# A fused attention and MLP block: the next chunk's normed rows are turned by VectorE's 32 by 32 blocks and DRAM transfers instead of TensorE transposes

## The chip, the cores and the metric

The kernel runs on one core of a Trainium2 chip. The metric is the device time of one execution in microseconds, lower is better, as the median of several runs. The profile and trace are of one further execution. Engines: TensorE (PE; its weight loads are PEld), VectorE (DVE), ScalarE (ACT), GpSimd (POOL), SyncE (SP), which here only issues DMA transfers.

## The reference

A sandwich-normed transformer block in float32: 16 sequences of 256 tokens, model width 256, 16 heads of 128, MLP width 2048. The MLP's weights come as four-bit codes with scales. Cut to what matters:

```python
def _layernorm(x, axis=-1, eps=1e-05):
    m = jnp.mean(x, axis=axis, keepdims=True)
    v = jnp.var(x, axis=axis, keepdims=True)
    return (x - m) / jnp.sqrt(v + eps)

# attention
q = jnp.einsum('bpd,hde->bphe', x, W_Q) + b_Q          # k, v alike
scores = jnp.einsum('bqhe,bkhe->bhqk', q, k) / ATTN_SCALE
attn = jax.nn.softmax(jnp.where(causal, scores, IGNORE), axis=-1)
out = jnp.einsum('bqhe,hed->bqd', jnp.einsum('bkhe,bhqk->bqhe', v, attn), W_O) + b_O
# MLP
Wg, Wu, Wd = (dequant_nvfp4(packed, scales) for each of gate, up, down)
gate, up = xt @ Wg.T, xt @ Wu.T
out = (gelu_tanh(gate) * up) @ Wd.T
# block
x = x + _layernorm(_L0_attn_ref(_layernorm(x, axis=-1), ...), axis=-1)
x = x + _layernorm(_L0_ffn_ref(_layernorm(x, axis=-1), ...), axis=-1)
```

## The kernel before

**Tiling.** The 4096 tokens are 8 chunks of 512 (two sequences each). All chunks pass through attention first, then all through the MLP; between them each chunk's result x1 lies in DRAM (`x1_scratch`, written from the tile `stream`). Every float32 product is three float32r products, hi x hi, hi x lo and lo x hi, so each operand is split: ACT writes the hi part (a rounded copy), DVE or POOL the lo part (value minus hi). Each projection of one head on one chunk is 6 matmuls of 512 columns (L752 to L754, helper `three`).

**Steps.** Attention is 128 steps, n = 16 c + j: chunk c, head j. `step_plan(n)` is the order in which TensorE works in a step: q and k of head n+1, the output projection of head n-3 ("out"), the weighted values of head n-2 ("z"), the scores of head n+1; and in steps with j % 4 = 1 the four banks of V (v0 to v3) for the next four heads. Such a step is called a V step here, the others short. ACT, DVE and POOL follow the same list with their own halves, each engine strictly in its order. The PSUM banks of q, k, z and v are three in a ring (`fbank`): a product can only start when the one three places before it has been split.

**The way of the probabilities.** After softmax (masks by DVE, exponentials by ACT, reciprocals by DVE, scaling by POOL), DVE turns head n's probabilities in 32 by 32 blocks ("T", line 1134, tile `turned`). SP sends `turned` to DRAM (`send`, L514), waits until it has landed, and loads it back as four DMAs in a turned layout (`fetch`, L524, tile `back`). In step n+1 ACT makes the hi part of it ("pT", L708, tile `pT_hi`) and only then the exponentials of head n+2, since its list says so; the lo part is POOL's, and TensorE uses both in step n+2. SP has one list for all transfers and stands still at each wait.

**Work hung between.** Around the steps DVE does other things in the gaps, set by tables: `X1_AT` for the norm and residual of the chunk before (its result `given` is turned by DVE blocks and by a DRAM round trip too, SP's `turn_given` at j = 5), `NEXT_AT` for the norm of the next chunk's rows (`norm_next_x`), and `spread` for the decoding of one piece of MLP weights in the steps named in `W4_SLOTS` (48 pieces in all; ACT, POOL and SP take part, with four DMAs in the step after). A place (j, "sum") is after step j's scores have been masked and z split and the sums inverted; (j, "end") is after the last V bank.

**The next rows before.** The rows of chunk c+1 are loaded to `x_in` (SP, j = 3 and 5), get their statistics at j = 10 and 12 and are normed into `stream` at (13, "end"), which has to wait until SP's stores of x1 out of `stream` (j = 11 and 13) have landed. In step 14 TensorE transposes them ("xT", L771: two groups of four transposes of 128x128 into PSUM, one before and one after "out"), ACT writes `xnT_hi` (L620) and DVE `xnT_lo` (L932). The q projection in step 15 reads them.

## Time and profile before

| | |
|---|---|
| median of 3 runs | 1577.87 us (1573.5 to 1579.29) |
| the profiled execution, whole time | 1580.88 us |
| its span in the trace | 1579.1 us |
| PE busy | 1549.9 us, 98% |
| DVE, ACT, POOL busy | 1071.8, 981.7, 711.2 us |
| DMA | 183.13 MB, mean 116 GB/s |

The attention steps take up the first 1040 us or so of the span, the MLP the rest. The profiled execution took 1580.88 us, 3.0 us above the median of the timed runs; 1.8 us of it lie outside the span. Matmuls overlap: one of 512 columns is shown with 0.39 us, but the next one starts 0.23 us after it, so lengths of PE work are read here from starts.

### The profile page before, as it was taken

The page shows a single profiled execution, that of the slowest core. Times are in us where ns is not written, and L with a number is a line of the kernel's source. Part 1 is how long each engine was busy: PE and PEld are TensorE (multiplying, and loading weights), DVE is VectorE, ACT ScalarE, POOL GpSimd, SP SyncE. Part 2 cuts the span into 40 slices and gives each one's busy share as a digit, 9 for nine tenths or more (in the row PEclk, how much of TensorE's full clock was granted, in tenths as well). Part 3 has the DMA queues.
Part 4 walks back from the last instruction along what each step waited for, and adds up shares of the span by engine and source line. Part 5 has one row for each costly group of instructions (what it writes and reads, how often), then busy time and mean ns, then how long its engine had stood idle before and what let it go on. Part 6 is the DMA issues. An engine that isn't in the chain of part 4 may idle for free.

```text
span 1579.1 us, 25677 instructions
## 1 busy us (share of the span) xinstructions
PE 1549.9 (98%) x8160; PEld 1332.4 (84%) x8160; DVE 1071.8 (68%) x3088; ACT 981.7 (62%) x2449; POOL 711.2 (45%) x1069
## 2 busy tenths in 40 slices
PE   6999999999999999999999999999999999999998
PEld 5888888888888888888888888887888888888887
DVE  5666677677777778667767766756666566565665
ACT  6887667767776776777776776653444444444443
POOL 5774445445554545445544543333333333333333
PEclk9999999999999999999999999999999999999999
DMA  4653444444454354444444455481101101111001
GB/s 135 188 169 114 142 137 145 146 155 137 139 173 134 124 172 135 145 156 131 141 152 144 146 162 159 155 289 52 43 26 54 41 28 42 38 54 41 27 28 40
DMA packets 168375, 183.13 MB, mean 116 GB/s; under 512 B 17328, under 2 KB 139696, under 8 KB 168240
## 3 DMA queue, kind: packets, MB, share of 16 engines
q1 hardware_dynamic: 168240, 181.50, 36.0%
q8 instruction: 65, 1.06, 0.3%
q14 instruction: 70, 0.57, 0.1%
HBM read 102.26 MB, written 79.17 MB: 115 GB/s over the span
## 4 chain that ended last, share of the span: by engine, by line
PE 79%; DMA 7%; SPq 4%; DVE 4%; ACT 4%; issue 2%; POOL 1%; DVEq 0%
PE fbank L752 13%; PE fbank L754 13%; PE fbank L753 13%; PE obank L752 6%; PE obank L754 6%; PE obank L753 6%; PE ubank L752 5%; PE ubank L754 5%; PE ubank L753 5%; DMA turned_scratch<-turned 3%; PE ubank L776 3%; PE fbank L854 2%; SPq L524 2%; DMA back<-turned_scratch 2%; ACT probs L640 1%
## 5 line engine op out<-in xcount | busy, mean ns | idle before, releaser
L752 PE MATMUL fbank<-xnT_hi,wqk_hi 128*128 128x512 f32 x768 | 301.2, 392 | 1.1 <-DVE xnT_lo L932 1.1
L753 PE MATMUL fbank<-xnT_lo,wqk_hi 128*128 128x512 f32 x768 | 300.2, 391 | 0.0
L754 PE MATMUL fbank<-xnT_hi,wqk_lo 128*128 128x512 f32 x768 | 299.8, 390 | 0.0
L1327 POOL TENSOR_TENSOR pT_lo<-back,pT_hi 128x512 fp32r<-128x512 f32 x128 | 165.8, 1295 | 290.6 <-ACT pT_hi L708 290.6
L651 ACT ACTIVATE w_raw<-fbank 128x512 f32<-128x512 f32 x128 | 76.5, 598 | 230.6 <-PE fbank L754 230.5
L1289 POOL TENSOR_SCALAR probs<-probs,rsum 128x128 f32<-128x128 f32 (+1 forms) x512 | 208.8, 427 | 14.5 <-DVE rsum L955 10.5
L947 DVE CUSTOM_DVE_ANT_0 probs<-ubank,mask 128x128 f32<-128x128 f32 (+1 forms) x512 | 155.9, 355 | 25.3 <-PE ubank L754 24.1
L754 PEld LDWEIGHTS fbank<-xnT_hi,wqk_lo 128*128 128x128 f32 x768 | 144.7, 188 | 30.8
L752 PEld LDWEIGHTS fbank<-xnT_hi,wqk_hi 128*128 128x128 f32 x768 | 145.4, 189 | 28.7 <-DVE xnT_lo L932 1.5
L753 PEld LDWEIGHTS fbank<-xnT_lo,wqk_hi 128*128 128x128 f32 x768 | 145.0, 189 | 25.7
L1307 POOL TENSOR_TENSOR v_lo<-probs,v_hi 128x512 fp32r<-128x512 f32 x64 | 82.4, 1288 | 166.0 <-ACT v_hi L660 166.0
L1071 DVE SCALAR_TENSOR_TENSOR probs<-w_raw,fbank 128x512 f32<-128x512 f32 x128 | 88.1, 688 | 98.3 <-ACT w_raw L655 95.9
L621 ACT ACTIVATE zT_hi<-fbank,bias_v 128x512 fp32r<-128x512 f32 x128 | 87.4, 683 | 101.8 <-PE fbank L854 101.8
L1065 DVE SCALAR_TENSOR_TENSOR w_raw<-w_raw,fbank 128x512 f32<-128x512 f32 x128 | 87.7, 685 | 86.9 <-ACT w_raw L651 85.8
L1307 POOL TENSOR_TENSOR kT_lo<-probs,kT_hi 128x512 fp32r<-128x512 f32 x64 | 82.9, 1296 | 134.1 <-ACT kT_hi L660 134.1
L934 DVE SCALAR_TENSOR_TENSOR kT_lo<-fbank,bias_k,kT_hi 128x512 fp32r<-128x512 f32 x128 | 95.9, 749 | 54.3 <-ACT k_early L632 53.6
L1134 DVE STREAM_TRANSPOSE turned<-probs 128x384 f32<-128x384 f32 x256 | 131.6, 552 | 0.6 <-DMA turned_scratch<-turned 0.6
L640 ACT ACTIVATE probs<-probs,nmax 128x256 f32<-128x256 f32 x256 | 126.7, 495 | 0.0
L655 ACT ACTIVATE w_raw<-w_raw 128x512 f32<-128x512 f32 x128 | 80.9, 632 | 47.6 <-DVE w_raw L1065 47.6
L955 DVE RECIPROCAL rsum<-sums 128x2 f32<-128x2 f32 x256 | 41.7, 163 | 100.2 <-ACT probs L640 99.7
L776 PE MATMUL ubank<-k_early,q_early 128*128 128x128 f32 x512 | 102.2, 281 | 7.2 <-DVE kT_lo L934 6.5
L638 ACT ACTIVATE probs<-probs,nmax 128x128 f32<-128x128 f32 x256 | 100.3, 392 | 9.8 <-DVE nmax L947 6.7
(144 smaller groups left out, 4288.4 us busy)
## 6 DMA issues: line engine op xcount, KB each, us to landing
turned_scratch<-turned SPq DMA_DIRECT2D x128, 384.0 KB, 2.6
back<-turned_scratch SPq DMA_DIRECT2D x512, 96.0 KB, 2.2
w_raw<-in_w_pairs SPq DMA_DIRECT2D x28, 256.0 KB, 3.0
w_hi_scratch<-w_hi SPq DMA_DIRECT2D x48, 128.0 KB, 2.0
w_lo_scratch<-w SPq DMA_DIRECT2D x48, 128.0 KB, 2.0
x_res<-in_x SPq DMA_DIRECT2D x16, 256.0 KB, 2.9
wqk_hi<-w_hi_scratch SPq DMA_DIRECT2D x16, 256.0 KB, 5.5
wqk_lo<-w_lo_scratch SPq DMA_DIRECT2D x16, 256.0 KB, 5.9
```

The lines of the kernel that those rows point to most:

```text
L638: act.activation(pr[:, 0:P], pr[:, 0:P], ACT.Exp, bias=nmax[:, 0:1], scale=-1.0, accum_out=sums[:, 0:1])
L640: act.activation(pr[:, P:384], pr[:, P:384], ACT.Exp, bias=nmax[:, 1:2], scale=-1.0, accum_out=sums[:, 1:2]).then_inc(s.exp, 1)
L752: nc.tensor.matmul(out, a[0], b[0], start=start, stop=False, skip_group_check=skip)
L753: nc.tensor.matmul(out, a[0], b[1], start=False, stop=False, skip_group_check=skip)
L754: return nc.tensor.matmul(out, a[1], b[0], start=False, stop=stop, skip_group_check=skip)
L776: nc.tensor.matmul(bank[:, 0:P], mem.q_early[i][:, b, :], mem.k_early[i][:, b, :], start=True, stop=True)
L934: ins = dve.scalar_tensor_tensor(dst, bank, bias, hi.bitcast(F32), ALU.add, ALU.subtract)
L947: last = dve.tensor_tensor_reduce(out=pr[:, lo:hi], in0=bank[:, lo:hi], in1=mask, scale=-SCALE, scalar=3.0e38, op0=ALU.add, op1=ALU.min, a ...
L1134: dve.transpose(mem.turned[:, :, :, b, :].rearrange("p k u j -> p u k j"), mem.probs[b].rearrange("p (u k j) -> p u k j", u=3, k=4)).then_ ...
L1289: last = pool.tensor_scalar(pr[:, lo:hi], pr[:, lo:hi], mem.rsum[i][:, at:at + 1], 1.0, ALU.mult, ALU.mult)
L1307: pool.tensor_tensor(lo, mem.act_v[j % 2], hi.bitcast(F32), ALU.subtract).then_inc(s.iT_lo, 1)
L1327: pool.tensor_tensor(lo[:].rearrange("p u b (a j) -> p (u b) a j", j=32), mem.back[m % 2][:, :, 0:2].rearrange("p a u b j -> p (u b) a j") ...
```

## The change

- The next chunk's rows are loaded earlier (both halves at j = 0), get their statistics at (1, "mid") and (2, "sum") and are normed in place in `x_in` at (4, "sum") and (5, "mid"), where "mid" is a new place between two V banks. In chunk 0 the first statistics are at (1, "end").
- At (6, "sum") DVE turns the normed rows in 32 by 32 blocks (`turn_rows`, four transposes of 128x256, whose source is read at a stride of two elements) into `w_raw` (chunk 0: `stream`). At j = 7 SP stores them to DRAM (512 KB), waits for the landing and loads them back to `x_in` as four DMAs of 128 KB. In step 14, after k, ACT writes `xnT_hi` and DVE `xnT_lo` from there; on DVE these two stand before T. TensorE's "xT" groups and their places in the ring of banks are gone from the attention steps. (The MLP's own transposes stay, and so do the eight of the kernel's start.)
- `turn_given` moves from j = 5 to j = 9 on SP, and `X1_AT` from places 3 to 9 to places 8 to 14; the x1 stores move from j = 11 and 13 to j = 15, both residual loads to j = 1 of the next chunk (the last chunk: j = 15).
- `W4_SLOTS` loses slot 15: seven pieces of MLP weights a chunk, so that the 48 reach into the last chunk; the loads of finished pieces wait for their own piece only.
- In the MLP's first chunk the parts of the attention's last norm and the roots that go with it stand one step later; the next rows' norm takes two steps instead of four.

The diff, cut to its core:

```diff
-W4_SLOTS = [1, 3, 5, 7, 9, 11, 13, 15]
-X1_ROOTS, NEXT_ROOTS = 9, 13
+W4_SLOTS = [1, 3, 5, 7, 9, 11, 13]
+X1_ROOTS, NEXT_ROOTS = 13, 3
...
     if n % HEADS == HEADS - 2:
-        plan += [("xT", 0)]
+        plan.insert(2, ("rows", n // HEADS + 1))
     if n > 2:
         plan += [("out", n - 3)]
-    if n % HEADS == HEADS - 2:
-        plan += [("xT", 1)]
     if n > 1:
...
+        self.first_stored = sem("first_x1_stored")
+        self.rows_turned = sem("rows_turned")
+        self.rows_sent = sem("turned_rows_stored")
+        self.rows_back = sem("turned_rows_back")
+        self.rows_hi = sem("rows_hi")
+        self.rows_lo = sem("rows_lo")
...
 def x1_norm(c):
-    return 2 * c + 2
+    return 2 * c + 3
 def next_norm(c):
-    return 2 * c + 3
+    return 2 * c + 2 if c else 3
...
-def load_program(sp, mem, s, x_v, w_pairs, biases, words_v, scales_v, w4_v, x1_v, turned_v, given_v, out_v):
+def stored_chunks(engine, s, chunks):
+    if chunks:
+        engine.wait_ge(s.first_stored, 32)
+    if chunks > 1:
+        engine.wait_ge(s.stored, 32 * (chunks - 1))
+def load_program(sp, mem, s, x_v, w_pairs, biases, words_v, scales_v, w4_v, x1_v, turned_v, given_v, rows_v,
+                 out_v):
...
-        sp.wait_ge(s.w4_stored, 32 * PIECES)
+        sp.wait_ge(s.w4_stored, 32 * (2 * unit + 2))
...
         if c:
-            sp.wait_ge(s.xn, c)
+            sp.wait_ge(s.rows_lo, KT * c)
         else:
         if c == NCH - 1:
-            sp.wait_ge(s.stored, 32 * (NCH - 2))
+            sp.wait_ge(s.first_stored, 32)
         src = part_of(x_v, c + 1, i) if c < NCH - 1 else part_of(x1_v, 0, i)
...
-                     mem.stream[:, i * half:(i + 1) * half]).then_inc(s.stored, 16)
+                     mem.stream[:, i * half:(i + 1) * half]
+                     ).then_inc(s.stored if c > 1 else s.first_stored, 16)
...
+    def turn_rows(n):
+        sp.wait_ge(s.rows_turned, 2 * n + 2)
+        if n:
+            sp.wait_ge(s.rows_back, 64 * n)
+        sp.dma_start(rows_v.rearrange("a i k c -> (a i) k c"),
+                     mem.rows_turned[min(n, 1)].rearrange("p k t r i -> p k (t r i)")
+                     ).then_inc(s.rows_sent, 16)
+        sp.wait_ge(s.rows_sent, 16 * (n + 1))
+        for k in range(4):
+            sp.dma_start(mem.rows_back[32 * k:32 * k + 32].rearrange("p a t r i -> p a (t r i)"),
+                         rows_v[:, :, k].rearrange("a i c -> i a c")).then_inc(s.rows_back, 16)
...
-        if c and j == 5:
+        if j == 7:
+            turn_rows(c)
+        elif c and j == 9:
...
                 w4_load(done + 1)
-        if j in (3, 5):
-            next_x(c, (j - 3) // 2)
-        elif c and j in (11, 13):
-            store_x1(c, (j - 11) // 2)
+        if j == 0:
+            for i in range(2):
+                next_x(c, i)
+        elif c and j == 1:
+            for i in range(2):
+                load_res(c - 1, i)
         elif j == 15:
-            load_res(c, 0)
-            if c == NCH - 1:
-                load_res(c, 1)
-        elif c and j == 1:
-            load_res(c - 1, 1)
+            for i in range(2):
+                if c:
+                    store_x1(c, i)
+                if c == NCH - 1:
+                    load_res(c, i)
         if c == NCH - 1 and j % HG == 1:
...
                 full(count, mem.zT[0][:], bank, mem.bias_v[:, h:h + 1]).then_inc(s.hi, 1)
-            else:
-                full(count, mem.xnT[0][:, m, :], bank).then_inc(s.hi, 1)
+        elif kind == "rows":
+            act.wait_ge(s.rows_back, 64 * m)
+            act.wait_ge(s.full, nth(("k", n + 1)))
+            for kt in range(KT):
+                act.activation(mem.xnT[0][:, kt, :].rearrange("p (t a i) -> p t a i", a=4, i=BLK),
+                               mem.rows_back[:, :, :, kt, :].rearrange("p a t i -> p t a i"),
+                               ACT.Copy).then_inc(s.rows_hi, 1)
         elif kind == "pT":
...
             act.wait_ge(s.out, m // HEADS + 1)
+            stored_chunks(act, s, m // HEADS)
             for i in range(2):
...
             if kind == "q" and h == 0:
-                pe.wait_ge(s.lo, split(("xT", m // HEADS, KT - 1)))
+                pe.wait_ge(s.rows_lo, KT * (m // HEADS))
             project(bank, h, 0 if kind == "q" else 1)
-        elif kind == "xT":
-            if m == 0:
-                pe.wait_ge(s.xn, c + 1)
-            transpose_x(mem.stream, m, bank).then_inc(s.full, 1)
         elif kind == "v":
...
         view = mem.given_turned[0 if n < NCH - 1 else 1]
-        if i == 0 and n == 0:
-            dve.wait_ge(s.w_split, len(PAIRS))
+        if i == 0 and n < NCH - 1:
+            dve.wait_ge(s.rows_sent, 16 * (n + 2))
         dve.transpose(view[:, :, :, i, :].rearrange("p a t j -> p t a j"),
...
             moments()
+        elif part == 5:
+            turn_rows(c)
         else:
             dve.wait_ge(s.rstd, next_norm(c))
-            if c:
-                dve.wait_ge(s.stored, c * 32)
-            last = standardise(xn, x_in, 2 * (part - 3))
-            if part == 4:
-                last.then_inc(s.xn, 1)
+            after(standardise(x_in, x_in, 2 * (part - 3)))
+    def turn_rows(n):
+        if n == 1:
+            dve.wait_ge(s.w_split, len(PAIRS))
+        for t in range(TT):
+            last = dve.transpose(mem.rows_turned[min(n, 1)][:, :, t].rearrange("p k r i -> p r k i"),
+                                 x_in[:, t, :].rearrange("p (k j r) -> p r k j", r=KT, j=BLK))
+            if t % 2:
+                last.then_inc(s.rows_turned, 1)
...
-    X1_AT = {(3, "sum"): (-2,), (4, "sum"): (-1,), (6, "sum"): (0,), (8, "sum"): (1, 2),
-             (9, "end"): (3, 4, 5, 6)}
-    NEXT_AT = {(10, "sum"): (0,), (12, "sum"): (1, 2), (13, "end"): (3, 4)}
+    X1_AT = {(8, "sum"): (-2, -1), (10, "sum"): (0,), (12, "sum"): (1, 2), (13, "mid"): (3, 4),
+             (14, "sum"): (5, 6)}
+    NEXT_AT = {(1, "mid"): (0,), (2, "sum"): (1, 2), (4, "sum"): (3,), (5, "mid"): (4,),
+               (6, "sum"): (5,)}
+    FIRST_NEXT_AT = {**NEXT_AT, (1, "end"): (0,)}
+        for part in (NEXT_AT if c else FIRST_NEXT_AT).get((j, place), ()):
+            norm_next_x(part, c)
-        for part in NEXT_AT.get((j, place), ()):
-            norm_next_x(part, c)
...
                     extra(c, j, "sum")
-            else:
-                full(count, mem.xnT[1][:, m, :], mem.xnT[0][:, m, :], bank)
+        elif kind == "rows":
+            for kt in range(KT):
+                dve.wait_ge(s.rows_hi, KT * (m - 1) + kt + 1)
+                dve.tensor_tensor(mem.xnT[1][:, kt, :].rearrange("p (t a i) -> p t a i", a=4, i=BLK),
+                                  mem.rows_back[:, :, :, kt, :].rearrange("p a t i -> p t a i"),
+                                  mem.xnT[0][:, kt, :].bitcast(F32).rearrange(
+                                      "p (t a i) -> p t a i", a=4, i=BLK),
+                                  ALU.subtract).then_inc(s.rows_lo, 1)
         elif kind == "T":
...
-            for part in {4: (-1,), 7: (0, 1), 8: (2, 3), 9: (4, 5)}.get(m, ()):
+            for part in {4: (-1,), 8: (0, 1), 9: (2, 3), 10: (4, 5)}.get(m, ()):
-        if 7 <= j < 11 and c < NCH - 1:
-            norm_next_y(j - 7, c)
+        first = 7 if c else 9
+        if j in (first, first + 1) and c < NCH - 1:
+            for part in (0, 1):
+                norm_next_y(2 * (j - first) + part, c)
...
                 w4_lo(piece)
+            if j == NEXT_ROOTS:
+                roots(next_norm(c))
             if c and j == X1_ROOTS:
                 roots(x1_norm(c))
-            if j == NEXT_ROOTS:
-                roots(next_norm(c))
         elif kind == "pT":
```

SP's list around the turned rows, chunk 1, from the last DMA of step 6 to the first of step 8's weight piece (`turned_scratch<-turned` is a send, `back<-turned_scratch` a fetch). Before:

```order
L500 DMA scale<-in_scales 128x1x128
L514 DMA turned_scratch<-turned 128x768
L524 DMA back<-turned_scratch 32x4x192 x4
L514 DMA turned_scratch<-turned 128x768
L524 DMA back<-turned_scratch 32x4x192 x4
L506 DMA w_hi_scratch<-w_hi 128x256
```

And in the changed kernel:

```order
L521 DMA scale<-in_scales 128x1x128
L535 DMA turned_scratch<-turned 128x768
L545 DMA back<-turned_scratch 32x4x192 x4
L566 DMA rows_scratch<-w_raw 128x1024
L571 DMA x_in<-rows_scratch 32x4x256 x4
L535 DMA turned_scratch<-turned 128x768
L545 DMA back<-turned_scratch 32x4x192 x4
L527 DMA w_hi_scratch<-w_hi 128x256
```

The store and the four loads of the rows now stand between the fetch of head 7 and the send of head 8.

DVE's list in step 14 of chunk 1, from q's lo part to the first mask of the scores. Before:

```order
L934 SCALAR_TENSOR_TENSOR qT_lo<-fbank,bias_q,qT_hi 128x256
L934 SCALAR_TENSOR_TENSOR kT_lo<-fbank,bias_k,kT_hi 128x512
L1134 STREAM_TRANSPOSE turned<-probs 128x3x4x32 x2
L932 TENSOR_TENSOR xnT_lo<-fbank,xnT_hi 128x512 x2
L947 ISA probs,nmax<-ubank,mask 128x128
```

And in the changed kernel:

```order
L975 SCALAR_TENSOR_TENSOR qT_lo<-fbank,bias_q,qT_hi 128x256
L975 SCALAR_TENSOR_TENSOR kT_lo<-fbank,bias_k,kT_hi 128x512
L1180 TENSOR_TENSOR xnT_lo<-x_in,xnT_hi 128x512 x2
L1190 STREAM_TRANSPOSE turned<-probs 128x3x4x32 x2
L988 ISA probs,nmax<-ubank,mask 128x128
```

The two lo parts of the next rows moved ahead of the turning of head 14's probabilities.

## Rows read from the trace of the kernel before

**Rows 1.** The page's first part: busy time, share, instructions by engine.
```profile
PE 1549.9 (98%) x8160; PEld 1332.4 (84%) x8160; DVE 1071.8 (68%) x3088; ACT 981.7 (62%) x2449; POOL 711.2 (45%) x1069
```

**Rows 2.** Timeline, PE: start us, length, engine, line, op, tiles, shape, count.
```profile
128.02 0.39 PE L752 MATMUL fbank<-xnT_hi,wqk_hi 128*128 128x512 f32 x1
...
130.75 0.63 PE L771 MATMUL fbank<-ident,stream 128*128 128x128 f32 x4
...
135.39 0.40 PE L752 MATMUL fbank<-xnT_hi,wqk_hi 128*128 128x512 f32 x1
...
1019.41 0.39 PE L752 MATMUL fbank<-xnT_hi,wqk_hi 128*128 128x512 f32 x1
```

**Rows 3.** Timelines of PE, DVE, SP's queue and ACT, chunk 7 steps 9 to 11.
```profile
976.49 0.40 PE L752 MATMUL fbank<-xnT_hi,wqk_hi 128*128 128x512 f32 x1
...
988.35 0.39 PE L752 MATMUL fbank<-xnT_hi,wqk_hi 128*128 128x512 f32 x1
...
993.02 1.03 DVE L1134 STREAM_TRANSPOSE turned<-probs 128x384 f32<-128x384 f32 x2
...
994.08 0.32 SPq L514 DMA_DIRECT2D turned_scratch<-turned  x1
...
994.75 0.39 PE L752 MATMUL fbank<-xnT_hi,wqk_hi 128*128 128x512 f32 x1
...
996.47 1.75 SPq L524 DMA_DIRECT2D back<-turned_scratch  x4
...
1000.78 0.62 ACT L708 ACTIVATE pT_hi<-back 128x512 fp32r<-128x512 f32 x1
```

**Rows 4.** The page's DMA issues: count, KB each, median us from issue to landing.
```profile
back<-turned_scratch SPq DMA_DIRECT2D x512, 96.0 KB, 2.2
```

**Rows 5.** Waits: engine, tile, line, releaser: total us, times, longest.
```profile
DVE stream L970 <- DMA x_scratch<-stream: 8.0, 7, 2.0
```

**Rows 6.** A group of DVE by form: count | busy us, mean ns | idle before.
```profile
L1134 DVE STREAM_TRANSPOSE turned<-probs 128x384 f32<-128x384 f32 x256 | 131.6, 552 | 0.6 <-DMA turned_scratch<-turned 0.6
```

**Rows 7.** Timeline of SP's queue, chunk 1: `turn_given` at step 5, then head 6.
```profile
192.12 0.42 SPq L533 DMA_DIRECT2D given_scratch<-w_raw  x1
195.16 1.73 SPq L537 DMA_DIRECT2D w_raw<-given_scratch  x4
...
197.59 0.34 SPq L514 DMA_DIRECT2D turned_scratch<-turned  x1
201.34 1.74 SPq L524 DMA_DIRECT2D back<-turned_scratch  x4
```

**Rows 8.** Timelines of ACT and PE, chunk 1, V step 5 with a late `back`.
```profile
186.71 0.63 ACT L708 ACTIVATE pT_hi<-back 128x512 fp32r<-128x512 f32 x1 [0.90 <-DMA back<-turned_scratch]
...
190.36 0.50 PE L752 MATMUL fbank<-wv_hi,xnT_hi 128*128 128x512 f32 x1
```

**Rows 9.** PE after three idle times; three windows: us, PE busy, PEclk, DMA share, GB/s.
```profile
37.62 0.80 PE L776 MATMUL ubank<-k_early,q_early 128*128 128x128 f32 x2 [2.01 <-DVE kT_lo L934]
...
975.23 0.49 PE L776 MATMUL ubank<-k_early,q_early 128*128 128x128 f32 x2 [1.34 <-DVE kT_lo L934]
...
1075.04 0.61 PE L752 MATMUL obank<-v_hi,wv_hi 128*128 128x512 f32 x1 [2.28 <-POOL v_lo L1307]
...
38.00:40.00 2.00, 2.00 (x11) 0.50 0.65 210
40.00:42.00 2.00, 2.00 (x8) 0.76 0.82 222
...
976.00:978.00 2.00, 2.00 (x13) 1.00 0.49 197
```

**Rows 10.** Timeline of DVE, first MLP chunk: the attention's last norm.
```profile
1070.32 1.54 DVE L987 BATCH_NORM_STATS2 stats<-back 128x6 f32<-128x256 f32 x4 [3.54 <-DMA back<-given_scratch]
```

**Rows 11.** Timelines of SP's queue and DVE, chunk 0, steps 0 and 1.
```profile
26.78 1.75 SPq L524 DMA_DIRECT2D back<-turned_scratch  x4
...
31.66 1.03 DVE L1134 STREAM_TRANSPOSE turned<-probs 128x384 f32<-128x384 f32 x2
```

More of the change, by code:

```diff
@@ L149, in full_key @@
 def full_key(n, kind, m):
-    if kind == "xT":
-        return (kind, n // HEADS + 1, m)
     if kind == "v":
@@ L281, in __init__, with blocks @@
                              for v in places]
+        def blocks(view):
+            return view.rearrange("p (k t r i) -> p k t r i", t=TT, r=KT, i=BLK)
+        self.rows_turned = [blocks(self.stream[:].rearrange("p t d -> p (t d)")), blocks(raw)]
+        self.rows_back = blocks(self.x_in[:].rearrange("p t d -> p (t d)"))
         def bank(name, shape):
@@ L767, in project, with transpose_x @@
         last.then_inc(s.full, 1)
-    def transpose_x(src, kt, bank):
+    def transpose_x(kt, bank):
         for t in range(TT):
-            last = nc.tensor.transpose(bank[:, t * P:(t + 1) * P], src[:, t, kt:D:KT], mem.ident[:])
+            last = nc.tensor.transpose(bank[:, t * P:(t + 1) * P], mem.x_in[:, t, kt:D:KT],
+                                       mem.ident[:])
         return last
@@ L871, in tensor_program @@
             if m == 0:
-                pe.wait_ge(s.lo, split(("xT", NCH, KT - 1)))
+                pe.wait_ge(s.rows_lo, KT * NCH)
             if m < 2:
@@ L1111, in vector_program @@
             if whole(kind, m):
-                if m == TT - 1:
-                    extra(c, j, "end")
+                extra(c, j, "end" if m == TT - 1 else "mid")
                 continue
@@ L1336, in pool_program @@
             inter_lo(c * NT + m - 1, m - 1)
-            if m == (7 if c == 0 else 4):
+            if m == (8 if c == 0 else 4):
                 roots(y_norm(c))
-            elif j == 8 and c < NCH - 1:
+            elif j == (7 if c else 9) and c < NCH - 1:
                 roots(y_next_norm(c))
```

13 lines of the change are left out of this document (7 added, 6 removed).

## The prediction

> **What bounds the kernel now.** The busy shares come first: TensorE is busy 98% of the span [rows 1], so time can only be won by giving it less to do or by closing what is left of its gaps. Next come the starts of its steps in PE's timeline. A short step takes 994.75 - 988.35 = 6.40 us, a V step 988.35 - 976.49 = 11.86 [rows 3]. Step 14, with the transposes, takes 135.39 - 128.02 = 7.37 [rows 2]. A chunk without any waiting would be 12 x 6.40 + 4 x 11.86 + 0.97 = 125.2 us; it is (1019.41 - 128.02) / 7 = 127.3 [rows 2]. So each chunk loses 2.1 us to stalls, 15 us in seven chunks. The third thing to read is how close the other queues run behind TensorE. In step 10 of chunk 7 DVE ends T 5.70 us after the step's start, SP sends at 5.73, fetches from 8.12 to 9.87, and ACT begins pT_hi in the next step at 1000.78 - 994.75 = 6.03 [rows 3]. A fetch lands 2.2 us after its issue [rows 4]; the last of the four is issued at about 9.4, so `back` is there at 11.6, that is 5.2 in the next step: **0.8 us of slack** for the whole way through DRAM. In a short step ACT has nothing to spare behind pT_hi, so more delay than that reaches TensorE one step later, less the time by which k's lo part is early, which I estimate at 0.4 us from the starts of the scores.
>
> In a V step there is more room, since the V banks follow. In chunk 1 step 5 pT_hi came at 186.71, late by a landing, and the fourth V bank, which waits for the first to be split, at 190.36, 3.65 later [rows 8]. Undisturbed it begins six matmuls before the step's end. Twelve take 130.75 - 128.02 = 2.73 [rows 2], six 1.36, so it begins at 11.86 - 1.36 = 10.50. Hence pT_hi may be as late as **6.85** in a V step; beyond that TensorE stalls one for one.
>
> **The change, part by part** (against the profiled execution, 1580.9 us).
>
> *Transposes gone.* 7.37 - 6.40 = 0.97 us for the eight of a chunk [rows 2, 3], eight chunks: **-7.8**. The rows show about 0.12 us for each transpose. The Trainium skill (TensorE: Matmul & The Clock Gate, part 4 on PE-mode transpose) gives about 275 ns for one in a kernel's context; by that the 64 would be worth 17.6 us and the sum 9.8 us lower. The measurement decides, so 0.12 stands.
>
> *Norms spread evenly.* The wait of the norm for the landing of x1's stores (8.0 us of DVE in seven chunks [rows 5]) has no cause left, since the rows are normed in place; it stood just ahead of step 14. The double loads on DVE (a turn of `given` beside a spread) are parted. What stays are the pieces of weights, seven a chunk, with four DMAs each in SP's list. I take it that of 15 us some 5 stay: **-10**, bounds -4 and -13.
>
> *Step 14.* On DVE the two lo parts (128x512; in proportion to the 0.552 us of 384 columns [rows 6] some 0.7 us each) now precede T, so T and the masks are 1.3 us late, and with them the exponentials. Behind the masks follow two residual adds of the same size, 1.4 us. DVE idles 32% of the time [rows 1], 2.0 us of a short step, and I count half of it ahead of k's lo part: 1.3 + 1.4 less 1.0 leaves this late by some 1.2 to 1.7, less 0.4. I take **+0.8** a chunk, eight chunks **+6.4**, bounds +2 and +11.
>
> *Step 6.* Four block transposes of 256 columns. One of 384 takes 0.552 [rows 6]; in proportion 0.37, at most the same 0.55: 1.5 to 2.2 us. The same 1.0 of idle time takes most of it, and k has 0.4: nothing on TensorE, but T of step 7 ends up to 0.3 late.
>
> *Steps 7 to 9: SP's list.* This is the term that decides. `turn_rows` stands behind fetch 7 and ahead of send 8, and a short step has no time for it. Its price is that of `turn_given`, same bytes, same form: 195.16 - 192.12 = 3.04 us from the store's issue past its landing, 1.73 for four loads, and the send that follows closely behind such loads takes 201.34 - 197.59 = 3.75 until its fetch can start, where a quiet one takes 2.39 [rows 7, 3]. Before, this stood in V step 5, whose extra 5.45 us hid it. Now, from step 7's start: T 6.0, send, landed after 2.4 to 2.9 (step 6's weight piece is on the queue), fetch issued until 10.6, store, loads from 13.65 to 15.4. That is 9.0 in step 8, where the send was due at 5.73. Landed at 12.75, `back` there 3.5 later (1.75 of issues, 2.2 of landing, less one issue) at 16.2: 9.8 in step 9. All quiet it would be 8.6. Step 9 is a V step, so TensorE stalls at its fourth bank by 9.8 - 6.85 = 2.95, quiet by 1.75. I take 2.8, in eight chunks **+22.4**, bounds +14 and +27.
>
> *The clock behind that stall.* After idle times of 2.01 and 2.28 us TensorE worked at half its clock (0.50, which is 1.2 GHz; window 38 to 40), after 1.34 us it stayed at full (1.00, 2.4 GHz; window 976 to 978) [rows 9]. A gap of 2.7 us is on the falling side. The window 40 to 42 has a mean of 0.76, so the half clock ended at 41.0; 41.0 - 37.6 = 3.4 us at half cost 1.7 us. In seven of eight chunks: **+11.9**, bounds 0 and +13.6.
>
> *Last chunk.* At j = 9 `turn_given` meets four loads of finished weights, as at j = 5 before, where the send of head 6 was held up and the stall at 975.23 followed [rows 9]. It moves rather than goes; as I counted it among the 15, it comes back: **+2**.
>
> *MLP start.* DVE waited 3.54 us for `given` [rows 10]; POOL's roots waited for DVE and TensorE 2.28 us for POOL, then ran at half clock [rows 9]. One MLP step is 18 matmuls, 4.1 us, more than the wait. One step later it is gone: 2.4 + 1.7 = **-4.1**, bounds 0 and -4.1.
>
> *Kernel start.* In chunk 0 the first statistics stand at (1, "end"), ahead of T. Their rows are issued only after the fetch that ends at 28.5, two issues of 0.45, and a landing of some 3 us; T began at 31.66 [rows 11]. With 0.8 of statistics T comes 1.4 later, on a way that already stalls TensorE at 37.62: **+1.4**, bounds 0 and +2.
>
> **Sum.** -7.8 - 10 + 6.4 + 22.4 + 11.9 + 2 - 4.1 + 1.4 = +22.2: the profiled execution would be 1603.1. It lay 3.0 above the median of the runs, so the median goes to **1600 us**, 1.4% slower.
>
> **The rivals.**
>
> *The clock stays up.* For it: a third idle time, of 1.34 us, left it at full, and only two cases speak for the fall, both at other places. Against it: both were shorter than the gap here. Without the 11.9 the median is **1588**; with the quiet stall of 1.75 instead, 1580.
>
> *SP's list is no bound.* If the rows' round trip were hidden, say because `back` of head 8 has more slack than I read, the stall, the clock and the last chunk's collision fall out: 1600 - 22.4 - 11.9 - 2 = **1564**, and the change does what its name says. For it: the DMA engines are far from full (0.49 of their time in a window of the attention steps [rows 9]), and the same round trip cost nothing at step 5. Against it: SP waits for a landing, which more bandwidth doesn't shorten, and at step 5 the V banks hid it. The stall begins where `back` of head 8 is more than 6.85 - 5.2 = 1.65 us late; I count 9.8 - 5.2 = 4.6.
>
> *The turns are dear.* If the strided source doubles the four block transposes to 3 us, k's lo part is late by 1.9, TensorE stalls 1.4 us more in step 7 and the way to send 8 grows: +11 us, **1611**. No row shows a strided turn. The Trainium skill (SBUF - State Buffer, door 1 on the DMA port swizzle) says that float32 reads within a 16-byte line keep full bandwidth, and a stride of two elements stays within; by it the price is the lower one, which is the one I took.
>
> **How the numbers follow.** Forecast (stall and half clock) 0.50; clock stays up 0.25; SP no bound 0.13; turns dear 0.12. The forecast with its own bounds reaches from about 1590 to 1609. The range takes in the clock rival and half of the dear turns: 1581 to 1611; what is left out is mostly the fast case. Within 0.5% of before (about what a measurement of this kernel can tell from no change) is 1570 to 1586: a part of the clock rival with quiet landings, 0.08. Faster 0.13, slower 0.79.
>
> **What would show it.** In the changed trace: SP's queue sends head 8 about 3 us later than 5.73 after step 8's start, in every chunk; ACT's pT_hi in step 9 waits for `back` near 9.8; the fourth V bank of step 9 has 2.5 to 3 us of idle time before it, released by DVE's v_lo, with PEclk at 0.50 behind it, eight times; step 14 is 6.4 long and step 15 about 7.2; the wait on x1's stores is gone and the idle time near 1075 too. I am wrong if pT_hi of step 9 starts before 6.9, or if the clock stays at 1.00 behind the stalls, or if new waits stand elsewhere, such as in step 7 by the turns.

## The result, and the profile after

| | before | after |
|---|---|---|
| median of four runs, us | 1578.58 (1573.50 to 1580.58) | 1608.49 (1603.62 to 1609.48) |
| profiled execution, whole / span, us | 1580.88 / 1579.1 | 1603.62 / 1601.8 |
| mean granted clock of TensorE | 0.996 | 0.992 |

The ratio is 1.0188, with a 95% interval of 1.0156 to 1.0220: the change costs 25 to 35 us. Its profiled execution was the fastest of its four; the spans of the two traces differ by 22.7 us.

The page of the changed kernel, first and fourth part (busy times, and the chain that ended last):

```profile
PE 1550.4 (97%) x8096; PEld 1327.8 (83%) x8096; DVE 1082.2 (68%) x3120; ACT 981.6 (61%) x2449; POOL 718.9 (45%) x1069
...
PE 67%; DMA 12%; SPq 6%; ACT 6%; DVE 5%; issue 2%; POOL 0%; DVEq 0%; ACTq 0%
```

TensorE has 64 matmuls fewer than in [rows 1] and as much busy time, because some of its matmuls ran at half clock. Transfers (DMA) and SP's queue (SPq) now hold 18% of the chain, which was 11% before. PE's waits (engine, tile, line, releaser: total us, times, longest) say where:

```profile
PE fbank L796 <- DVE v_lo L973: 21.5, 10, 3.3
PE ubank L821 <- DVE kT_lo L975: 9.8, 15, 4.3
```

A V bank waited for `v_lo` ten times, 21.5 us in all; before, no row of this view had that wait. One of the ten, from step 7 to step 9 of chunk 1 (steps begin at 205.09, 211.50 and 217.91), in the timelines of PE, SP's queue and ACT:

```profile
205.09 0.39 PE L796 MATMUL fbank<-xnT_hi,wqk_hi 128*128 128x512 f32 x1
...
211.50 0.39 PE L796 MATMUL fbank<-xnT_hi,wqk_hi 128*128 128x512 f32 x1
...
217.91 0.39 PE L796 MATMUL fbank<-xnT_hi,wqk_hi 128*128 128x512 f32 x1
...
231.75 0.50 PE L796 MATMUL fbank<-wv_hi,xnT_hi 128*128 128x512 f32 x1 [2.73 <-DVE v_lo L973]
```

```profile
210.82 0.32 SPq L535 DMA_DIRECT2D turned_scratch<-turned  x1
213.33 3.30 SPq L545 DMA_DIRECT2D back<-turned_scratch  x4
216.72 0.38 SPq L566 DMA_DIRECT2D rows_scratch<-w_raw  x1
219.48 1.73 SPq L571 DMA_DIRECT2D x_in<-rows_scratch  x4
221.31 0.38 SPq L535 DMA_DIRECT2D turned_scratch<-turned  x1
224.48 1.73 SPq L545 DMA_DIRECT2D back<-turned_scratch  x4
```

```profile
228.10 0.63 ACT L751 ACTIVATE pT_hi<-back 128x512 fp32r<-128x512 f32 x1 [4.07 <-DMA back<-turned_scratch]
```

Step 7 takes 211.50 - 205.09 = 6.41 us and head 7 is sent 5.73 into it: the turns on VectorE delay nothing. In step 8 SyncE fetches head 7, stores the rows, stands for their landing until 219.48, issues four loads, and sends head 8 at 221.31, which is 9.81 after the start of step 8. `back` releases pT_hi at 228.10, 10.19 into step 9, and the fourth V bank starts 3.65 later, as in [rows 8]: 3.34 us late.

The differences between the two traces' starts of TensorE's steps, summed over the chunks, against the terms of the prediction ("late T" is its term for step 14):

| steps | the prediction's terms, us | measured, us |
|---|---|---|
| 14 to 1 of the next chunk | -7.8 transposes, +6.4 late T: -1.4 | -1.4 (14 and 15: -6.5; 0 and 1: +5.1) |
| 4 to 13 | -10 spread, +22.4 stall, +11.9 clock, +2 last chunk: +26.3 | +22.7 (4 to 8: -6.4; 9 and 10: +29.0) |
| kernel start | +1.4 | +3.0 |
| MLP | -4.1 | -1.6 |
| sum | +22.2 | +22.7 |

The clock. PE in chunks 2 and 5, and windows (us, PE busy, PEclk, DMA share, GB/s) behind the stalls of chunks 1, 2 and 5:

```profile
363.03 0.50 PE L796 MATMUL fbank<-wv_hi,xnT_hi 128*128 128x512 f32 x1 [2.58 <-DVE v_lo L973]
...
752.57 0.50 PE L796 MATMUL fbank<-wv_hi,xnT_hi 128*128 128x512 f32 x1 [3.29 <-DVE v_lo L973]
```

```profile
232.00:234.00 2.00, 2.00 (x7) 0.58 0.52 150
...
363.00:365.00 2.00, 1.97 (x9) 1.00 0.52 149
365.00:367.00 2.00, 2.00 (x10) 1.00 0.71 263
...
754.00:756.00 2.00, 2.00 (x10) 1.00 0.93 338
```

TensorE fell to 1.2 GHz behind the idle time of 2.73 us and stayed at 2.4 GHz behind one of 2.58, and in chunk 5 behind one of 3.29. In this execution it fell in four of eight chunks, for 3.4 us each time, which costs 1.7.

The kernel start (DVE, then PE), step 14 of chunk 1 (PE, then DVE), and the MLP (DVE, PE, POOL):

```profile
33.37 0.75 DVE L1001 BATCH_NORM_STATS2 stats<-x_in 128x6 f32<-128x256 f32 x2 [3.01 <-DMA x_in<-in_x]
...
40.12 0.80 PE L821 MATMUL ubank<-k_early,q_early 128*128 128x128 f32 x2 [4.35 <-DVE kT_lo L975]
```

```profile
265.93 0.39 PE L796 MATMUL fbank<-xnT_hi,wqk_hi 128*128 128x512 f32 x1
...
272.34 0.46 PE L796 MATMUL fbank<-xnT_hi,wqk_hi 128*128 128x512 f32 x1
...
270.76 1.42 DVE L1180 TENSOR_TENSOR xnT_lo<-x_in,xnT_hi 128x512 fp32r<-128x512 f32 x2
272.10 1.02 DVE L1190 STREAM_TRANSPOSE turned<-probs 128x384 f32<-128x384 f32 x2
```

```profile
1097.19 1.54 DVE L1028 BATCH_NORM_STATS2 stats<-back 128x6 f32<-128x256 f32 x4 [1.76 <-DMA back<-given_scratch]
...
1115.91 0.47 PE L796 MATMUL obank<-v_hi,wv_hi 128*128 128x512 f32 x1 [1.45 <-POOL v_lo L1365]
...
1113.24 0.19 POOL L1312 TENSOR_SCALAR var_eps<-mv 128x4 f32<-128x4 f32 x1 [3.58 <-DVE mv L1006]
```

VectorE stood 3.01 us for the first rows, with head 1's T queued behind, and TensorE idled 4.35 us at 40.12 where it idled 2.01 before [rows 9]. Step 14 is 6.41 long instead of 7.37, but T ends at 273.12, 7.19 after its start. In the MLP the wait for `given` went from 3.54 [rows 10] to 1.76, and TensorE's stall at 1075 went with the half clock behind it; 0.53 us is left, at 1101.94. A new stall stands at 1115.91, where GpSimd stood for the moments of the next rows with TensorE's `v_lo` queued behind.

### The profile page after: what moved, and what is told of

Its sections match the earlier page's. It is cut to its first block, busy times and chain, and to the rows that moved or that the text cites. A ratio compares the mean times of both kernels' runs of the same rounds, so it can differ in the third digit from the quotient of the medians.

```text
span 1601.8 us, 25642 instructions
## 1 busy us (share of the span) xinstructions
PE 1550.4 (97%) x8096; PEld 1327.8 (83%) x8096; DVE 1082.2 (68%) x3120; ACT 981.6 (61%) x2449; POOL 718.9 (45%) x1069
## 4 chain that ended last, share of the span: by engine, by line
PE 67%; DMA 12%; SPq 6%; ACT 6%; DVE 5%; issue 2%; POOL 0%; DVEq 0%; ACTq 0%
PE fbank L796 12%; PE fbank L798 12%; PE fbank L797 12%; DMA turned_scratch<-turned 6%; PE obank L796 5%; PE obank L798 5%; PE obank L797 5%; PE ubank L798 4%; PE ubank L796 4%; PE ubank L797 4%; SPq L545 3%; DMA back<-turned_scratch 3%; PE ubank L821 2%; PE fbank L895 2%; ACT probs L678 2%
## 5 line engine op out<-in xcount | busy, mean ns | idle before, releaser
L1347 POOL TENSOR_SCALAR probs<-probs,rsum 128x128 f32<-128x128 f32 (+1 forms) x512 | 216.6, 444 | 21.8 <-DVE rsum L996 18.0
L988 DVE CUSTOM_DVE_ANT_0 probs<-ubank,mask 128x128 f32<-128x128 f32 (+1 forms) x512 | 155.3, 354 | 24.7 <-PE ubank L798 22.7
L797 PEld LDWEIGHTS fbank<-xnT_lo,wqk_hi 128*128 128x128 f32 x768 | 146.1, 190 | 26.3
L796 PE MATMUL fbank<-wv_hi,xnT_hi 128*128 128x512 f32 x256 | 102.2, 399 | 23.4 <-DVE v_lo L973 21.5
L751 ACT ACTIVATE pT_hi<-back 128x512 fp32r<-128x512 f32 x128 | 80.2, 626 | 58.3 <-DMA back<-turned_scratch 57.6
```

The lines of the kernel that those rows point to most:

```text
L796: nc.tensor.matmul(out, a[0], b[0], start=start, stop=False, skip_group_check=skip)
L797: nc.tensor.matmul(out, a[0], b[1], start=False, stop=False, skip_group_check=skip)
L988: last = dve.tensor_tensor_reduce(out=pr[:, lo:hi], in0=bank[:, lo:hi], in1=mask, scale=-SCALE, scalar=3.0e38, op0=ALU.add, op1=ALU.min, a ...
L1347: last = pool.tensor_scalar(pr[:, lo:hi], pr[:, lo:hi], mem.rsum[i][:, at:at + 1], 1.0, ALU.mult, ALU.mult)
```

## The experiments

Each time is a median with the ratio to the kernel before, run beside it.

**The loads one step later.** The changed kernel, with this edit. SyncE's wait for the landing moves too, as it stands just ahead of the loads.

```diff
                     ).then_inc(s.rows_sent, 16)
+
+    def rows_home(n):
         sp.wait_ge(s.rows_sent, 16 * (n + 1))
         for k in range(4):
...
             turn_rows(c)
+        elif j == 8:
+            rows_home(c)
         elif c and j == 9:
```

> The changed kernel, but SyncE stores the turned rows in step 7 as before and issues their four loads one step later, behind fetch 8, by when the store has long landed: nothing is left that SyncE waits for between fetch 7 and send 8. The same bytes move. If the landing that SyncE stands for (and the loads behind it) makes send 8 late, send 8 goes from 9.8 us after its step's start to about 5.8, step 9 of every chunk falls from some 15.3 us to 11.9, and 27.9 us of stall with the half clock behind it go, less what the loads in step 8 add to head 8's fetch (they stand behind it; up to 0.3 us a chunk for send 9): 1605 - 26 = about 1579 to 1582. The rival, that it is the added bytes or VectorE's added turns that make head 8 late, expects step 9 to stay above 14 us and the time above 1600.

1587.4 us, ratio 1.0043 (1.0029 to 1.0058). SP's queue, ACT and PE of chunk 1:

```profile
214.03 0.34 SPq L535 DMA_DIRECT2D turned_scratch<-turned  x1
...
222.39 0.63 SPq L535 DMA_DIRECT2D turned_scratch<-turned  x1
...
230.22 1.73 SPq L558 DMA_DIRECT2D w_raw<-given_scratch  x4
232.12 0.34 SPq L535 DMA_DIRECT2D turned_scratch<-turned  x1
236.50 1.73 SPq L545 DMA_DIRECT2D back<-turned_scratch  x4
```

```profile
239.97 0.63 ACT L755 ACTIVATE pT_hi<-back 128x512 fp32r<-128x512 f32 x1 [1.05 <-DMA back<-turned_scratch]
```

```profile
226.38 0.39 PE L800 MATMUL fbank<-xnT_hi,wqk_hi 128*128 128x512 f32 x1
...
245.26 0.49 PE L825 MATMUL ubank<-k_early,q_early 128*128 128x128 f32 x2 [0.66 <-DVE kT_lo L979]
```

Step 9 is 11.9 us in all chunks: the whole stall of step 9 went, with the bytes unchanged. So what SyncE does between fetch 7 and send 8, the wait and the four loads together, made it, and the rival (bytes, or the turns) is out. The time was forecast at 1579 to 1582 and is some 6 us longer, because the next wait came forward: steps 11 to 13 of chunks 1 to 7 are 12.5 us longer than before. The send of head 10 (232.12, 5.74 into step 10) goes right behind the loads of `given` and its fetch starts only 4.38 us later; that makes pT_hi late in step 11 and TensorE idle in step 12. In the changed kernel the stall of step 9 had hidden this: SyncE caught up meanwhile, and head 11 was sent 6.0 to 7.7 us into its step in chunks 1 to 7, where it is now 6.5 to 11.0.

**The wait alone.** The changed kernel again, but `sp.wait_ge(s.rows_sent, ...)` stays in step 7 and only the four loads go to step 8.

> The changed kernel, but with only the four loads of the turned rows moved to step 8: the store and SyncE's wait for its landing stay in step 7, ahead of send 8. It splits the price into landing and loads. If the delay adds up as the prediction has it, send 8 leaves at about 8.1 us of step 8 (9.8 less 1.7 of issues), nothing goes ahead of it in the queue (2.4 instead of 3.1 to land), so head 8 is back at 7.6 to 8.1 in step 9 instead of 9.2 to 10.4; with 6.85 tolerated the stall of step 9 falls from 3.5 to about 1.1 a chunk, without half clock behind it: about 20 us of the 27.9 gone, 1587. If the wait is the whole price and the loads cost nothing, the time stays near 1605; if the loads are the whole price, it falls to that of the kernel with both moved, 1580.

1591.8 us, ratio 1.0074 (1.0058 to 1.0090). Step 9 is 0.63 us a chunk too long (5.1 in eight) instead of 3.5. Send 8 of chunk 1 left 8.31 into its step, forecast 8.1; the others left at 6.6 to 8.1. So the wait by itself leaves a stall, if a small one, and the loads carry the rest: they come on top of a wait that has used up the tolerance. The time is above the forecast 1587 by the stalls of steps 11 to 13 (12.4 us), which are here too.

**T between the lo parts.** On top of the first experiment, in step 14 (`rows_low` is one lo part; TensorE's first projection of step 15 waits for each half by itself):

```diff
         elif kind == "rows":
-            for kt in range(KT):
...
+            rows_low(m, 0)
         elif kind == "T":
...
+            if n % HEADS == HEADS - 2:
+                rows_low(n // HEADS + 1, 1)
```

> The kernel with the loads in step 8, and in step 14 VectorE turns the head's probabilities between the two lo parts of the next rows instead of behind both; TensorE's first projection of step 15 then waits for each half by itself. T of step 14 then ends at about 6.5 us instead of 7.2. If T's lateness makes step 15 and the first two steps of the next chunk long (about 1.2 us a chunk by the two traces), 0.8 to 1.2 us a chunk go: 6 to 9 us less than the kernel with the loads moved alone. If the stalls there come from x1's stores and the row loads in SyncE's list in steps 15 and 0, the time stays within 2 us of that kernel. A new stall would be the wait for the second half: the projection reaches it 0.7 us into step 15 and it is there at about 0.75, so at most 0.3 us a chunk.

1580.8 us, ratio 1.0003 (0.9992 to 1.0014), 6.3 us less than without by the ratios. DVE's rows, step 14 from 259.61:

```profile
265.18 1.02 DVE L1197 STREAM_TRANSPOSE turned<-probs 128x384 f32<-128x384 f32 x2
266.13 0.64 DVE L1165 TENSOR_TENSOR xnT_lo<-x_in,xnT_hi 128x512 fp32r<-128x512 f32 x1
```

T ends at 6.59 instead of 7.19, and step 1, 5.9 us longer than before over seven chunks in the first experiment, is 1.1 longer. The term "step 14" is real. Its size is less sure than the 6.3 us look: step 1 alone is 3.6 to 6.6 us too long in the five traces without this edit and 1.1 to 3.8 in the six with it, so executions of like kernels differ there by almost as much as the edit gains.

**The transposes twice.** In the kernel before:

```diff
+            transpose_x(mem.stream, m, bank)
             transpose_x(mem.stream, m, bank).then_inc(s.full, 1)
```

> The kernel before the change with each of step 14's eight transposes of the next rows made twice into the same place (same result), in eight chunks 64 transposes more (56 in chunks 1 to 7 and 8 in chunk 0). This prices what the change takes off TensorE. At the 0.97 us a chunk read from the rows and no slack it is +7.8 us, 1586; by the figure of the Trainium skill's clock-gate page (275 ns for one at the warm clock) it would be +17.6, 1596. If TensorE's wait elsewhere in the step hid them, +0 to +2: then the change's gain from the transposes was not one either.

1587.4 us, ratio 1.0053 (1.0034 to 1.0073): +8.4 us. PE's rows, step 14 of chunk 0:

```profile
127.66 0.39 PE L752 MATMUL fbank<-xnT_hi,wqk_hi 128*128 128x512 f32 x1
...
128.35 1.11 PE L771 MATMUL fbank<-ident,stream 128*128 128x128 f32 x8
...
136.01 0.39 PE L752 MATMUL fbank<-xnT_hi,wqk_hi 128*128 128x512 f32 x1
```

Step 14 takes 8.35 us, with 7.37 before; over eight chunks step 14 grew by 8.7 us, 0.14 for a transpose. The interval (5 to 12 us) excludes 17.6. The profile has 285 ns as the mean duration of one of them, at full clock; they overlap, eight in 1.11 us. The expectation has the Trainium skill's 275 ns as a figure for full clock, where the page (TensorE: Matmul & The Clock Gate, part 4) gives it for one transpose in a kernel's context and doesn't tie it to the full clock. It is near the duration shown here, and twice the time that a transpose adds.

**The changed kernel again, for the clock.**

> The changed kernel once more, unchanged, for its clock. In its first profile the clock fell to half behind 4 of the 8 stalls of step 9 (2.53, 2.91, 2.68 and 2.37 us) and stayed at full behind the other four (2.75, 2.77, 3.45 and 2.73 us), so length alone doesn't order them. If it is the place (what TensorE does around the stall of that chunk), the same four chunks fall again, and the stalls are within 0.3 us of those before. If it is where the stall happens to lie in time against something that the program doesn't set, other chunks fall, between 2 and 6 of them, 1.7 us each; the span then is 1602 plus or minus 3.

The one run took 1613.7 us, span 1611.9. PE and windows (PE, PEld, DVE, ACT and POOL busy, then PEclk, DMA share, GB/s), chunks 2 and 3:

```profile
367.17 0.72 PE L796 MATMUL fbank<-wv_hi,xnT_hi 128*128 128x512 f32 x1 [2.68 <-DVE v_lo L973]
```

```profile
498.82 0.50 PE L796 MATMUL fbank<-wv_hi,xnT_hi 128*128 128x512 f32 x1 [2.52 <-DVE v_lo L973]
```

```profile
368.00:370.00 2.00, 2.00 (x6) 1.54 (x6) 1.15 (x6) 0.00 (x0) 0.57 (x2) 0.50 0.88 267
...
500.00:502.00 2.00, 2.00 (x11) 1.64 (x10) 0.84 (x4) 0.72 (x2) 0.92 (x3) 1.00 0.90 298
```

The clock fell in chunks 0, 1, 2, 5 and 7; in the first profile in 0, 1, 4 and 7. Chunk 2 fell here and not there, with idle times of 2.68 and 2.58. So the same place of the same program falls in one execution and not in another. This execution was 10 us longer than the profiled one, outside the plus or minus 3 that I gave it: steps 9 and 10 cost 3.2 more, of which 1.7 are the fifth half clock, step 1 3.0, steps 12 and 13 2.6. Part of it may be the place and time of the run: the kernel before, run beside it, took 1583.0, which is 4.4 more than beside the first result. A single run can't tell that from a spread of the chain through DRAM.

**First statistics in step 2.** The changed kernel, with this edit for chunk 0.

```diff
-    FIRST_NEXT_AT = {**NEXT_AT, (1, "end"): (0,)}
+    FIRST_NEXT_AT = {**NEXT_AT, (2, "sum"): (0, 1, 2)}
```

> The changed kernel, but in chunk 0 the first statistics of the next rows stand in step 2, with the others, instead of step 1 ahead of T. In the changed kernel VectorE stood 3.0 us there for its rows to land, and TensorE 4.5 us at 40.1 against 2.2 at 37.6 before. If that wait is the cause, T of step 1 ends 2.5 to 3 us earlier, the stall at the scores of head 3 is back at about 2.2 us, and with the half clock behind it 3 to 4 us of the start go (steps 0 to 3 take 3.6 less than in the changed kernel). If SyncE's two row loads in step 0 (behind fetch 0, ahead of send 1) are the cause, the stall stays above 3.5 us and less than 1.5 us go.

DVE and PE:

```profile
30.69 1.03 DVE L1190 STREAM_TRANSPOSE turned<-probs 128x384 f32<-128x384 f32 x2
...
37.77 0.49 PE L821 MATMUL ubank<-k_early,q_early 128*128 128x128 f32 x2 [1.36 <-DVE kT_lo L975]
```

T of step 1 starts at 30.69 instead of 34.15, the stall is 1.36 instead of 4.35, no half clock follows it, and steps 0 to 3 are 4.7 us shorter. VectorE's wait was the cause; the two loads in SyncE's list were not. The whole (one run, 1613.2 us) says nothing of 4.7 us, since steps 9 and 10 cost 4.8 us more than in the first profile, and steps 12 and 13 4.1 more. The clock fell in chunks 1, 3, 4 and 5 here, in chunk 1 for 6.8 us.

**Both round trips split.** On top of the turn between the lo parts: rows loaded in step 9; `given` stored in step 9, loaded in step 10, its statistics in step 11.

> The kernel with the turn between the lo parts, but the second round trip of the chunk is split as well: in step 9 SyncE issues the loads of the turned rows and the store of what attention gave; the four loads of the latter follow in step 10, behind fetch 10, and their statistics one step later, in step 11. In the two kernels with the rows' loads in step 8, the stalls came back in step 12 (7.6 to 8.7 us in seven chunks more than before), with head 10's send up to 7.7 us and its fetch 11.2 us after the step's start. If SyncE's standing for that second landing is the cause, steps 10 to 13 lose their stalls but for 2 us (7 to 9 us less, and in the last chunk, where four loads of finished weights meet it, 2 to 4 of these) and the time is about 1572. If the cause is the number of transfers in SyncE's list (the rows' loads plus the weight piece), the stalls stay and the time is that of the former kernel, 1581.

1584.0 us, ratio 1.0008 (0.9994 to 1.0022). The forecast of 1572 was wrong: steps 12 and 13 are 9.2 us longer than before in chunks 1 to 7; without the split, steps 11 to 13 were 9.7 longer. SP's queue in chunk 4, where step 11 starts at 612.75:

```profile
614.90 1.75 SPq L545 DMA_DIRECT2D back<-turned_scratch  x4
616.69 2.61 SPq L561 DMA_DIRECT2D w_raw<-given_scratch  x4
619.35 0.43 SPq L527 DMA_DIRECT2D w_hi_scratch<-w_hi  x1
...
621.56 0.40 SPq L535 DMA_DIRECT2D turned_scratch<-turned  x1
```

SyncE waits for no landing here, yet sends head 11 8.81 into its step: four loads and four issues for the weight piece stand behind one fetch. That fits the expectation's rival, the number of transfers in SyncE's list.

**All together.** The former, with the first statistics in step 2, and with the roots of the MLP's next rows and the second part of their norm a step later.

> All that the runs pointed to, on the changed kernel: both round trips split into store and, a step later, loads; T between the lo parts in step 14; chunk 0's first statistics in step 2; in the first chunk of the MLP the roots of the next rows one step later, so that GpSimd doesn't stand for the statistics that are made in that very step. Against the kernel without the last two: 3.5 us less at the start and 1.6 less in the MLP (the stall near 1093 to 1116), 1567 if the former is at 1572. If another wait stands behind those two, 1570 to 1572. It would be below the kernel before (1581 in that job) by 0.5 to 0.9%.

1580.4 us, ratio 0.9984 (0.9972 to 0.9996), 3.8 us less than the former by the ratios; its start is 4.2 shorter. The MLP part gained nothing (2.2 us below before in both traces): the stall of 1.3 us at the old place is gone, but TensorE now idles 0.49 us for `v_lo` at 1102.10 and 0.25 for `xnT_lo` at 1103.96. The 12 us between 1572 and 1584 were already lost in the former.

**The rows' loads in the V step, all of `given` there too.** On top of the turn between the lo parts.

> The kernel with the turn between the lo parts, but the four loads of the turned rows stand in step 9 (a V step) instead of step 8, ahead of the store, the wait and the loads of what attention gave, all in step 9. Where step 8 held the rows' loads and the weight piece, eight issues behind fetch 8, SyncE reached send 9 only at 7.9 to 9.1 us; now it should leave by 6.0. SyncE's last load of step 9 comes at about 17.4, which is 5.6 in step 10: send 10 is in time but queued behind loads (4 us to land instead of 2.4), as before. If the number of issues in step 8 mattered, the 9.6 us of steps 11 to 13 fall by a half, to 1576; if the chain starts at send 10 behind the loads, as the traces of step 10 suggest (back of head 10 at 6.6 to 7.3 in step 11), nothing changes: 1581.

1587.8 us, ratio 1.0057 (1.0043 to 1.0071): worse than both expectations, 8.5 us above that kernel. In chunk 3 the send of head 9 left at 6.56, the store landed 3.5 us after its issue, and the last load's issue ended 6.6 into step 10, so send 10 left at 6.72, a full microsecond late. In the last chunk, where four loads of finished weights stand in the same step, TensorE stalled 3.0, 1.1 and 1.8 us in step 12. A landing waited for and nine issues are too much for this V step too.

**The loads of `given` in step 11.** The kernel with everything, but with the MLP as in the changed kernel, and this edit. Step 11 has no weight piece to store or load.

```diff
-        elif c and j == 10:
+        elif c and j == 11:
             given_home(c - 1)
...
-    X1_AT = {(8, "sum"): (-2, -1), (11, "sum"): (0,), (12, "sum"): (1, 2), (13, "mid"): (3, 4),
+    X1_AT = {(8, "sum"): (-2, -1), (12, "sum"): (0, 1, 2), (13, "mid"): (3, 4),
```

> Both round trips split, with the loads put where SyncE has no weight piece to move: the rows' in step 9, those of what attention gave in step 11 (step 10 has the piece: two stores and two loads), its statistics all in step 12; T between the lo parts; first statistics in step 2. With the loads in step 10, SyncE made eight issues behind fetch 10 and sent head 11 at 7.6 to 8.8 us instead of 5.7, and the stalls of steps 12 and 13 stayed (10 to 12 us). If a short step holds no more than about four issues of 0.45 us behind its fetch (which ends at 10.2; the next send is due at 5.7 of the next step, which is 12.1), send 12 leaves by 6 and steps 11 to 13 lose 8 to 10 us: against the 1580 of the kernel with everything, 1571. If the stalls of step 12 come from VectorE's statistics and roots there, they stay or grow: 1580 or above.

**1570.0 us, ratio 0.9954 (0.9941 to 0.9968)**, forecast 1571: 7 us faster than the kernel before. SP's queue in chunk 3 (step 11 from 479.30, step 12 from 485.71):

```profile
487.46 1.75 SPq L545 DMA_DIRECT2D back<-turned_scratch  x4
489.55 1.74 SPq L561 DMA_DIRECT2D w_raw<-given_scratch  x4
491.60 0.34 SPq L535 DMA_DIRECT2D turned_scratch<-turned  x1
```

Send 12 leaves at 5.89. Steps 11 to 13 are 5.7 us longer than before instead of 11.7 in the kernel with everything; 5.2 of what is left stand in step 13. The statistics, which are now all made ahead of step 13's T, may be the cause, and so may the weight piece in SyncE's list; neither was tried.

**The next rows' loads in step 1.** On top of the former; the residual rows' loads go from step 1 to 3.

> The former kernel, and from chunk 1 on the loads of the next rows stand in step 1 (a V step) instead of step 0, their statistics all in step 2, and the residual rows are loaded in step 3 instead of step 1. It prices what steps 15 to 1 hold: head 0's trip goes behind x1's stores and these loads, and step 1 is 3.5 to 4 us too long over seven chunks. If the loads in step 0 are the cause, 3 us go; if x1's two stores in step 15 are, nothing does (within 1 us).

1575.1 us, ratio 0.9972 (0.9961 to 0.9983). Step 1 is 1.5 us longer than before over seven chunks, in the former kernel 1.6, so moving the loads out of step 0 brought nothing. But the 3.5 to 4 us that were to be explained (3.5 and 3.8 in the two kernels before) had already fallen to 1.6 without any edit there, so the test had little left to find. Steps 3 and 5 became 2.2 us longer; the residual loads behind a short step's fetch are the likely price. That x1's stores are the cause wasn't tried and stays open.

## Why the prediction was right, point by point

It forecast 1600 us, between 1581 and 1611, by 22.2 us of added time in the profiled execution; the median is 1608.5, and the profiled one has 22.7. The path that it named, SyncE's list, is the one that the traces show. That the sum came within 0.5 us is partly luck, since the misses of its terms cancel: in this execution the clock cost 5.1 less than forecast, the norms gained 1.0 more and the last chunk's +2 isn't seen, while step 14 cost 2.5 more, the stall 1.7 and the start 1.6, and the MLP gained 2.5 less.

*SP's list: right.* Send 8 was forecast at 9.0 in its step and left at 8.8 to 9.8, pT_hi forecast at 9.8 in step 9 came at 9.2 to 10.4, and the tolerance of 6.85 held to 0.01. What pT_hi is late beyond the tolerance sums to 24.1 us over the eight chunks, the idle time shown ahead of step 9's V banks to 21.7; the term was 22.4. The first two experiments show that the wait and the loads behind it make it. That `given` would be the next to be late wasn't in the prediction; the stall hid it.

*The clock: right in kind, too high for the traces.* The term said seven of eight chunks. Four fell in one traced execution and five in the other, each worth some 1.7 us, so 7 to 8.5 us instead of 11.9; the rival "the clock stays up" is as far off on its side. The other three timed executions have a mean granted clock of 0.989, 0.989 and 0.990 where the profiled one has 0.992, which is 3 to 5 us more lost to half clock; by that estimate (a thousandth is 1.6 us) two or three more chunks fell in them, six or seven in all. The step that failed is "a gap of 2.7 us is on the falling side": at 1.9 to 3.3 us of idle time no side exists that the program decides.

*Norms spread: nearly.* -10 was forecast; steps 4, 5 and 8 give -6.4, the 2.2 us that step 9 lost before are gone too, as the loads one step later show, and so are the 2.4 us that step 14 lost before in chunks 1, 3 and 4, where the norm waited for x1's stores: -11.0 in all. *Last chunk:* its +2 isn't visible beside the stall; it came in step 12 where the stall was away.

*Transposes and step 14: right in kind.* -7.8 is 8.7 by the doubling. +6.4 is 6.3 by T moved between the lo parts, but steps 15, 0 and 1 are 8.9 us longer in the changed kernel; the first row of the table agrees to the decimal only because this and the 2.4 us of the norms in step 14 cancel. The figure that I set against the rows (Trainium skill, TensorE: Matmul & The Clock Gate, part 4) isn't what a transpose costs in this stream. *The turns:* L1075's group has

```profile
L1075 DVE STREAM_TRANSPOSE w_raw<-x_in 128x256 f32<-128x256 f32 x28 | 9.8, 408 | 0.0
```

four times 0.41 us, in the bounds of 0.37 to 0.55. In the kernel before, turns of 384 and 512 columns take 552 ns and 693 ns:

```profile
L979 DVE STREAM_TRANSPOSE w_raw<-stream 128x512 f32<-128x512 f32 x14 | 9.7, 693 | 0.0
```

A straight line through these two gives 0.41 us for 256 columns, so the strided source costs nothing that can be seen, and that rival is out.

*Kernel start: mis-sized.* +1.4 counted a landing of 3 us against T's old time; T came 2.5 us later, the stall doubled and more half clock followed: +3.6 in steps 0 to 3, 0.6 of it given back before.

*MLP: mis-sized.* The stall at 1075 and its half clock did go, worth 3.6 of the 4.1 us; 0.53 is left at 1101.94. What the term missed is a new stall 14 us later, at 1115.91, which takes 1.7 back, where GpSimd waits for the moments of the next rows, whose norm now takes two steps instead of four; with smaller differences that makes -1.6. With these roots and the norm's second part a step later the stall only moved to later steps, so what it takes to lose it stays open.

*Why the median is 8.5 above:* the sum was made against an execution that lay 3.0 above its median; the changed kernel's profiled one lies 4.9 below its own, and the repeat was 10 above the profiled one. The clock explains most of the 4.9, by the estimate above. The spread itself is no wider than before: 5.9 us over the four executions of the changed kernel, 7.1 over the four of the kernel before.

*The rival "SP's list is no bound"* said 1564 for a hidden round trip. The kernel with both trips hidden behind free steps ran in 1570, but it also has T between the lo parts (6.3 us) and the first statistics later (some 4); without these it would be near 1580 by this estimate. So even with both trips out of SyncE's way the rival's sum is too low, in part because 5.7 us are left in steps 12 and 13.

## What to carry to other kernels

A queue that waits for a landing pays it with everything behind it: store in one step, load in a later one, and put the loads where that queue has little else to issue. Count issues as well as waits: here a short step of 6.4 us held a fetch and about four more transfers, at 0.45 us each. After taking a stall away, read what it had been hiding before adding up its worth.

## What the runs showed of the hardware that I had not expected

TensorE's clock is not decided by the length of an idle time in this range. Idle times of 2.68 and 2.58 us at the same place in two executions were followed by 0.50 and by 1.00; one of 3.29 us left the clock at full; and an idle time of 1.7 us in the last chunk's step 12 (1.73 to 1.75 in four kernels, 1.1 us of idle time shortly before it in each, and 3.0 before that where all loads stand in step 9) was followed by half clock with the loads in step 8 and with all loads in step 9, and by full clock with the wait alone in step 7 and with T between the lo parts. A stall of 2 to 3.3 us must be priced with a chance for the 1.7 us, not with a yes or no.

A send that directly follows four loads on the same queue takes longer until its fetch can start: 3.1 to 4.4 us behind the loads of `given` in the first experiment (4.38 from 232.12 to 236.50), 3.17 behind the rows' loads in chunk 1 of the changed kernel (221.31 to 224.48). A quiet one takes 2.4 [rows 3].
